# Batch 0 of a fused attention and FP4 feed-forward kernel: where the weight splits, the scales, the quantising of tiles and GpSimd's rounding stand among the steps

## The reference, cut to what matters

```python
xn = _layernorm(x)                                   # x: (8, 512, 512)
qkv = xn @ Wqkv_w.T + Wqkv_b                         # 16 q heads, 8 k heads, 4 v heads of 256
p = softmax(q1 @ k1.T) - lam * softmax(q2 @ k2.T)    # causal, differential attention
o = einsum('bhqk,bkhe->bqhe', p, v)
s = (o * rsqrt(mean(o*o) + EPS) * subln_w * (1 - LAMBDA_INIT)) @ out_w.T + out_b
a, w = quant_dequant_mxfp4(xn), quant_dequant_mxfp4(weight)   # blocks of 32, shared power of two
g = silu(a @ w.T + bias)
out = x + s * g
```

## Time and profile before

| | |
|---|---|
| median of 3 runs | 1618.49 us (1616.91 to 1618.52) |
| the profiled execution's own time | 1619.56 us |
| its span, first to last instruction | 1617.8 us |
| busy share of PE, DVE, ACT, POOL | 92%, 70%, 54%, 53% |

### The profile page before, as it was taken

The page is one execution under the profiler, slowest core; times in us unless marked ns, Lnnn a source line. Parts: engine busy times, 40 slices in busy tenths (PEclk is TensorE's granted clock), DMA queues, the critical chain, the costliest instruction groups (busy, mean ns, idle before and its releaser), DMA issues.

```text
span 1617.8 us, 27497 instructions
## 1 busy us (share of the span) xinstructions
PE 1485.5 (92%) x8956; PEld 866.4 (54%) x8972; DVE 1134.8 (70%) x2657; ACT 877.0 (54%) x2474; POOL 852.6 (53%) x1587
## 2 busy tenths in 40 slices
PE   4676878999899998999999998999999998999978
PEld 2343445456565565556564555555654555655644
DVE  6778677757777677757777578767777577775661
ACT  5456766346653566346663476436663466534651
POOL 2455445655455554655556555655546554554443
PEclk9888989999999999999999999999999999999999
DMA  8144543234433334234532344334442344323332
GB/s 260 38 102 92 114 84 68 47 98 81 84 63 95 79 61 94 64 85 86 97 73 47 96 82 88 65 98 73 79 88 54 93 85 89 69 59 77 67 72 72
DMA packets 382352, 134.23 MB, mean 83 GB/s; under 512 B 361856, under 2 KB 365952, under 8 KB 382208
## 3 DMA queue, kind: packets, MB, share of 16 engines
q1 hardware_dynamic: 382208, 132.46, 38.8%
HBM read 35.41 MB, written 8.39 MB: 27 GB/s over the span
## 4 chain that ended last, share of the span: by engine, by line
PE 51%; DVE 15%; ACT 12%; POOL 9%; issue 7%; DMA 4%; SPq 1%; ACTq 0%; POOLq 0%; DVEq 0%
PE ps L527 14%; PE ps L529 14%; PE ps L528 14%; ACT pp L694 4%; DVE ps L1004 3%; DVE qkv L962 3%; PE ps L598 2%; PE ps L596 2%; PE ps L597 2%; ACT qkv L671 2%; ACT ph L703 2%; DMA pT<-ph 2%; ACT on L716 1%; DMA out_x<-res 1%; DVE ph L1016 1%
## 5 line engine op out<-in xcount | busy, mean ns | idle before, releaser
L694 ACT ACTIVATE pp<-ps,row 128x384 f32<-128x384 f32 (+3 forms) x512 | 268.0, 524 | 294.4 <-DVE row L1004 293.1
L1208 POOL TENSOR_TENSOR row<-row,small 128x1 f32<-128x1 f32 x256 | 141.0, 551 | 422.7 <-ACT pp L694 422.7
L527 PE MATMUL ps<-xT,wqkv 128*128 128x512 f16 x768 | 294.7, 384 | 14.3 <-DVE wqkv L902 7.4
L1004 DVE CUSTOM_DVE_ANT_0 ps<-ps,mask,ssc 128x384 f32<-128x384 f32 (+3 forms) x512 | 280.3, 552 | 31.4 <-PE ps L598 29.7
L529 PE MATMUL ps<-xT,wqkv 128*128 128x512 f16 x768 | 294.3, 383 | 0.0
L528 PE MATMUL ps<-xT,wqkv 128*128 128x512 f16 x768 | 294.2, 383 | 0.0
L1016 DVE SCALAR_TENSOR_TENSOR ph<-pp,small,ph 128x128 f16<-128x128 f32 (+3 forms) x256 | 152.0, 594 | 121.6 <-ACT ph L703 119.4
L527 PE MATMUL ps<-qkv,pT 128*128 128x256 f16 x640 | 177.7, 278 | 54.1 <-DMA pT<-ph 52.4
L962 DVE SCALAR_TENSOR_TENSOR qkv<-ps,bsc,qkv 128x512 f16<-128x512 f32 x192 | 143.3, 749 | 101.8 <-ACT qkv L671 100.9
L703 ACT ACTIVATE ph<-pp,small 128x128 f16<-128x128 f32 (+3 forms) x256 | 141.4, 552 | 128.5 <-DVE pp L1010 126.7
L527 PE MATMUL ps<-wout,heads 128*128 128x512 f16 x512 | 194.3, 380 | 2.5 <-DVE qkv L962 1.7
(11 more groups left out here) (133 smaller groups left out, 2979.0 us busy)
## 6 DMA issues: line engine op xcount, KB each, us to landing
xres<-in_x SPq DMA_DIRECT2D x32, 256.0 KB, 3.5
out_x<-res SPq DMA_DIRECT2D x32, 256.0 KB, 2.3
wqkv<-in_wqkv SPq DMA_DIRECT2D x15, 512.0 KB, 6.6
xin<-in_x SPq DMA_DIRECT2D x7, 1024.0 KB, 5.9
vbias<-in_bv SPq DMA_DIRECT2D x32, 128.0 KB, 3.2
pT<-ph SPq DMA_TRANSPOSE x256, 2.7
wout<-in_ow SPq DMA_DIRECT2D x7, 512.0 KB, 4.5
heads<-on SPq DMA_TRANSPOSE x128, 3.2
```

Source lines behind the costliest of these rows:

```text
L527: mm(out, ah, bh, start=start and j == 0, stop=False)
L694: run(out, sc_ps[u][:, m, 0:w], ACT.Exp, bias=ebias[:, u, m:m + 1], scale=-1.0, accum_out=psum_l[:, n % 6, m:m + 1]).then_inc(exp_done, 1)
L1004: nc.vector.tensor_tensor_reduce(sc, sc, mask[:, S - w:S], ssc[:, c:c + 1], BIG, ALU.add, ALU.min, ebias[:, u, m:m + 1]).then_inc(max_done, 1)
```

## The change

It touches only the setup and batch 0, apart from two waits.

- Each weight's low part (`w_low`, `o_low`) is done by DVE one step after ACT's high part, ahead of `normalised_lo`, where before both stood at the end of one step. The high parts move too: those of Wqkv by up to two steps in either direction, and those of out_w up to two steps earlier.
- The four parts of a tile are no longer done two per step in ten steps: ops 0 to 3 stand in one step and ops 4 and 5 two steps later (`TILE_AT`). Tiles 1 (its second half) to 7 are in steps 1 to 15; the setup does 6 parts in place of 12.
- POOL rounds a tile one step after DVE's ops 0 to 3, behind its small operations for the softmax.
- `norms` is no fill any more: it stands in `attend`, writes the unused half of an output bank, and comes at steps 4, 8 and 20 in place of 5, 11 and 23. The squares it sums are asked for at steps 3, 7 and 20. DVE copies its result in the step after.
- The layer norm of batch 1 moves from steps 9 to 12 to steps 15 to 18 on DVE; POOL's root is one step behind DVE's statistics, in the same step as ACT's use of it. The high parts of x move to steps 17 to 20.
- In the setup ACT does all four layer norms first, DVE all four low parts of x, and PE runs ten extra matmuls ("warm") ahead of fill 0; `norm 1` stands behind fill 0.
- The feed-forward weight is loaded into `heads`, not `gate`. The last out_w tile is loaded twice, once for its square and once for its split.

```diff
-X_STEP = 5
+X_STEP = (6, 5)
...
-SQ_STEP = {8: 0, 9: 1, 10: 2, 11: 3, 12: 6, 13: 7, 14: 8, 15: 9, **{WT + p: 13 + p for p in range(OP - 1)}, WT + OP - 1: 21}
-LOAD_O = {**{p: 10 + p for p in range(OP - 1)}, OP - 1: 19}
-NORM_STEP = {2: 5, 3: 11, 4: 23}
-W_SPLIT = {5: 0, 6: 1, 7: 3, 8: 6, 9: 7, 10: 9, 11: 11, 12: 13, 13: 14, 14: 15, 15: 17}
+SQ_STEP = {8: 0, 9: 0, 10: 1, 11: 2, 12: 4, 13: 5, 14: 5, 15: 6, **{WT + p: 12 + p for p in range(OP)}}
+LOAD_O = {p: 9 + p for p in range(OP)}
+SUM_STEP = {3: 3, 7: 4, 20: 5}
+NORM_STEP = {4: 3, 8: 4, 20: 5}
+W_SPLIT = {5: -1, 6: 1, 7: 3, 8: 5, 9: 7, 10: 9, 11: 10, 12: 12, 13: 13, 14: 15, 15: 17}
+OUT_SPLIT = {0: 22, 1: 23, 2: 24, **{p: 23 + p for p in range(3, OP)}}
...
+TILE_AT = {1: (None, 1), 2: (1, 3), 3: (3, 5), 4: (7, 9), 5: (9, 11), 6: (11, 13), 7: (13, 15)}
...
-AQ_STEP = WQ_STEP[NT - 1] + 2
-OUT_SPLIT = {p: 24 + p for p in range(OP)}
+AQ_STEP = WQ_STEP[NT - 1] + 1
...
-SETUP = [("norm", 0), ("norm", 1), ("fill", 0), ("fill", 1), ("fill", 2), ("fill", 3), ("fill", 4),
+SETUP = [("norm", 0), ("warm", 10), ("fill", 0), ("norm", 1), ("fill", 1), ("fill", 2), ("fill", 3), ("fill", 4),
...
                 wait(pe, on_lo, n - 1)
+                if n in NORM_STEP:
+                    norms(junk[u], NORM_STEP[n])
...
+                for t in range(5, WT):
+                    if W_SPLIT[t] == n - 1:
+                        w_low(t)
+                for p in range(OP):
+                    if OUT_SPLIT[p] == n - 1:
+                        o_low(p)
+                if n - 1 in NORM_STEP:
+                    dve.wait_ge(on_hi, n)
+                    take(junk[(n - 1) % 2], 4)
                 if n:
                     normalised_lo(n - 1)
...
-                if b == 0:
-                    for t in range(5, WT):
-                        if W_SPLIT[t] == s:
-                            w_low(t)
...
                 for c in range(SETUP_PARTS, 32) if b == 0 else ():
-                    if c % 4 == 1 and part_at(c)[0] == s:
+                    if c % 4 == 1 and part_at(c)[0] == s - 1:
...
-                for k in norm_at(b, s) if b + 1 < B else ():
+                for k in norm_at(b, s if b else s - 1) if b + 1 < B else ():
```

More of the change, by code:

```diff
@@ L390, in load_w, with load_o @@
                 sp.dma_start(w_src(t), wqkv_d[t].rearrange("p a n -> p (a n)")).then_inc(ld_w[t], 16)
[L392 to L396, removed]
+            def load_o(p, src):
+                sp.dma_start(src, ow_d[p].rearrange("p m n -> p (m n)")).then_inc(ld_ow[p], 16)
             sp.dma_start(bcol, bcol_d).then_inc(ld_small, 16)
@@ L429, in _ @@
                 load_w(t)
[L430 to L432 removed]
+            sp.dma_start(wq, fw_d.rearrange("(k p) h -> p k h", p=P)).then_inc(ld_fw, 16)
             for t in range(8, 12):
@@ L477, in _ @@
                     if LOAD_O[p] == s:
-                        load_o(p)
-                if s == X_STEP and b + 1 < B:
+                        load_o(p, o_sum(p))
+                if n == AQ_STEP + 3:
+                    for j in range(2):
+                        sp.wait_ge(aT_done[j], 16)
+                    load_o(OP - 1, o_src(OP - 1))
+                if s == X_STEP[b > 0] and b + 1 < B:
                     sp.wait_ge(q_done, (b + 2) * NT if b else NT)
@@ L730, in layer_norm @@
                     .then_inc(xn_done, 1)
[L732 to L735, removed]
+            for k in range(NT):
+                layer_norm(k, k)
+                x_hi(k)
             square(0)
+            square(1)
             act.wait_ge(su_lam, 1)
             run(lamv[:, 2:4], lamv[:, 0:2], ACT.Exp).then_inc(su_exp, 1)
-            for k in (2, 3):
-                layer_norm(k, k)
-                x_hi(k)
             w_high(0)
-            for t in range(1, 4):
-                square(t)
+            square(2)
+            square(3)
             w_high(1)
@@ L766, in _ @@
             fill(FIRST[7])
+            w_high(5)
             for n in range(NSTEPS):
@@ L875, in o_squares, with take, scales @@
                 nc.vector.tensor_copy(wnorm[:, 17:18], bsum[:, 16:17]).then_inc(su_in, 1)
-            def scales(i, sums, free=None):
+            def take(sums, count):
+                link(nc.vector.tensor_copy(bound[:, 0:count], sums[:, 0:count]))
+            def scales(i):
                 lo, hi = ((0, 1), (1, 4), (4, 8), (8, 12), (12, 16))[i]
-                link(nc.vector.tensor_copy(bound[:, 0:hi - lo], sums))
-                if free is not None:
-                    nc.vector.memset(apart, 0.0).then_inc(free, 1)
                 power_scale(scl[:, lo:hi], bound[:, 0:hi - lo], 10, half=4)
@@ L973, in fill @@
                     tt(bank, bank, fbias[:], ALU.add).then_inc(biased, 1)
[L974 to L979, removed]
-                        o_scales(bank[:, 0:2])
                 elif kind == "last" and LAST_PIECES[j][g][1] < OC:
@@ L1050, in _ @@
                 layer_norm(k, k, 0)
+            for k in range(NT):
+                x_lo(k)
+            squares(0)
             dve.wait_ge(ld_lam, 16)
@@ L1077, in _ @@
             fill(FIRST[1])
+            w_low(3)
+            fill(FIRST[2])
             quantise_early(1)
-            w_low(3)
-            for m in range(2, 5):
-                fill(FIRST[m])
-                quantise_early(2)
+            fill(FIRST[3])
+            quantise_early(1)
+            fill(FIRST[4])
             maxima(0, 1)
@@ L1094, in _ @@
             dve.wait_ge(su_norm, 3)
-            scales(2, ps[:, 6, 0:4])
+            take(junk[0], 4)
+            scales(2)
             score_scales(1)
@@ L1128, in _ @@
                         gating(f)
+                if SUM_STEP.get(n) == 5:
+                    o_squares()
+                elif n in SUM_STEP:
+                    squares(SUM_STEP[n])
                 prepare(b, s, "maxima")
+                for t in range(5, WT):
[7 more added lines that the diff above has]
+                    take(junk[(n - 1) % 2], 4)
                 if n:
                     normalised_lo(n - 1)
+                if n - 1 in NORM_STEP:
+                    if n < 16:
+                        scales(NORM_STEP[n - 1])
+                        score_scales(NORM_STEP[n - 1] - 1)
+                    else:
+                        o_scales()
                 for f in PLAN[n]:
```

80 lines of the change are left out of this document (39 added, 41 removed).

## The result

The changed kernel takes 1607.26 us (median of 5 runs, 1603.83 to 1612.23) against 1618.49 (5 runs, 1615.47 to 1620.75) before: a ratio of 0.9937, 95% interval 0.9913 to 0.996. It is faster by 11.2 us, where 22 were forecast. The profiled execution took 1606.69 us, with a span of 1604.9.

What follows compares the result with a forecast made beforehand. PE bounds the kernel overall, but hand-overs between DVE, ACT and POOL bound batch 0. Setup -11, steps 0 to 15 -12, steps 16 to 21 +8, steps 22 to 31 -7: -22 us, median about 1596, own range 1586 to 1603, whole 1584 to 1609.

Steps and rivals of the forecast that it cites:

- steps 16 to 21: Batch 0, where DVE and ACT work arrives and ACT waits for POOL's root: +8 us, from +4 to +12.
- the setup: Everything until step 0: earlier fill 0, less tile work, a shorter scale chain; -11 us, from -7 to -14.
- steps 22 to 31: Batch 0's end: `o_scales` leaves and 5 of 8.0 us of waits for `o_high` go; -7 us, from -2 to -10.
- steps 0 to 15: Batch 0's first steps: mainly less DVE idle time; -12 us, from -4 to -18.
- the +2: Steps 0 to 15: two more POOL rounds in the loop stretch DVE operations beside them, +2 us.
- +3.3 and -1.1: Steps 16 to 21, ACT's work: four layer norms and a high part of x arrive (+3.3 us), a square leaves (-1.1).
- I expect only 2.5 us of this: Setup: fourth low part of x comes about 4.9 us earlier, of which 2.5 us is gained; bounds 0 and 4.9.
- I take +1.5: Setup: `norm 1` behind fill 0 on PE, with `w_low(1)` and fill 2 behind it, costs 1.5 us; bounds 0 and 5.
- -5.5 + 1.5: Setup: tile 1's quantising leaves its place ahead of the first scores (-5.5 us); `norm 1` behind fill 0 costs +1.5.
- -4.5: Setup, 44.57 us to step 0: ops 0 to 3 replace a whole tile (-1.5), round after the scale chain (-3).
- Rival 3: Loop: a round and a `w_low` lock each other in seven steps, 1.3 us each; +9, 1605 us; chance 0.08.
- Rival 1: Loop: waits only change place, only the setup's -11 remains; 1607 us, from 1603 to 1611; chance 0.17.

Runs made afterwards that it cites:

- the second run with later bias loads: Changed kernel with layer norm a step later, norm 1 first, two more warm matmuls, bias loads behind x's transposes, bias wait at fill 6: 1596.36 us (0.9854).
- the first run with later bias loads: Changed kernel with layer norm a step later, norm 1 first, eight more warm matmuls, bias loads behind x's transposes: 1598.96 us (0.9888).

## Why the prediction was off, step by step

The mechanisms of the sum were mostly right, and sizes failed: steps 16 to 21 cost 15.8 us, not 8, the setup gave 6.4 us, not 11, and steps 22 to 31 gave 10.6, not 7.

**Right.** That the page's 92% hides a batch 0 whose bound is the hand-overs between DVE, ACT and POOL, and that time saved there is not given back later: the part behind batch 1 changed by 0.9 us. That steps 0 to 15 lose 12 us: they lost 12.5. DVE was idle 13.3 us in them (106.54 - 93.20), against 13.4 forecast from the 0.84 us a step of steps 16 to 21. DVE operations beside a round were stretched by 6.3 us in all in these steps, and by 4.2 before (what each takes beyond the same operation away from a round, summed), as the +2 had it. The two mechanisms behind the gain were shown one at a time: the low parts' hand-over (8.6 us of the stretch when undone) and the rounds (7.9). Together this is more than the 12.5, so they overlap. Of the sum's four terms, only this one ended within its bounds; the setup (-6.4) and steps 22 to 31 (-10.6) missed theirs by 0.6 us each, steps 16 to 21 by 3.8. A setup of the same code varied by 1.4 to 1.6 us, so its 0.6 means little.

**"Steps 16 to 21 ... it will also wait in four steps for POOL's root ... some 1 us each, half of it hidden. I take +6.5 + 1.5 = +8."** This term failed by its size: +15.8, outside its bound of +12. The wait was 2.0 us each (7.9 in four), and taking the hand-over apart gave back 5.4 us of the stretch, where the sum had 1.5 for it. I had counted it on ACT alone; but the high part of x stands behind the layer norm, and DVE's low part of x in the same step behind that, so DVE stood still too (6.3 us) and began the next step late. With the hand-over a step later, the stretch took 40.5 us, near the 38.2 that the sum gives. This is 5.4 of the 7.8 us that the term was off. For the rest there is ACT's work: it rose by 5.9 us in the stretch (25.28 to 31.20), where I had +3.3 and -1.1. Four squares of weight tiles stand in it before and after, so that none was lost, and the high part of one more Wqkv tile now falls inside its bounds. That this is what the last 2.4 us are is how I read it, and no run tells it apart.

**"I expect only 2.5 us of this (bounds 0 and 4.9)."** Fill 0 came 0.35 us earlier. DVE's fourth low part did come 4.8 us earlier, at 11.87, but what counts is the transpose behind it. SP in the changed kernel:

```profile
9.86 9.23 SPq L434 DMA_TRANSPOSE xT<-gate  x2
```

The first was issued at 9.86 and landed 9.4 us later, behind the loads in the queues. Its issue alone kept SP for 7.3 us (4.3 with the bias loads behind it), and the second was issued at 17.2 only, nearly as late as before (17.4), to land 4.4 us later. I had moved the transpose on the engine that asks for it and not on the queue that carries it. Moving the bias loads behind it brought the landing to 18.5 us, though step 0 gained only 0.5 of this.

**"`norm 1` now stands behind fill 0 ... I take +1.5, with bounds 0 and 5."** It cost 2.5 us, and fill 0 at the lower clock another 1.7, as the two runs on it showed. The warm matmuls, which I gave nothing in the sum, gave nothing that shows; with PE idle for 4.1 us behind them, fill 0 was slow all the same.

In these executions the 4.6 us missing from the setup lie in three places: 2.2 at the start of fill 0; 1.4 between it and the first scores (-2.6 in place of -5.5 + 1.5); and 1.0 from there to step 0 (-3.5 in place of -4.5), where a 4-column operation of the scale chain still takes 1.00 us (L839 at 49.68), now beside POOL's low part of v.

**"A round stretches what DVE does beside it ... +2."** This was about right (4.2 us before, 6.3 after). Rival 3, full blocking at every `w_low`, did not come about, but its mechanism was hardly put to the test: of eleven in the loop, one took 2.35 us, beside the round of step 0, 1.07 more than the other ten with 1.28, which is near the 1.3 of the rival. Those in a step with a round came some 2.4 us before it (69.13 and 71.54, 83.06 and 85.46) and did not meet it.

**"Steps 22 to 31: -7."** It was -10.6, just outside the bound of -10. The step that failed is "so I count 5 of them": I had set 5 of 8 us for the eight waits for `o_high`. Undoing the hand-over costs 6.4 us there, and the kernel before with it alone gains 8.9.

**Rival 1** (the waits only change place) comes nearest in time, 1607, but by the wrong sum: the loop did gain, 7.3 us, and the setup gave 6.4, not 11. Its mechanism was in part there: against the 20.1 us of waits that went, the one in `p_lo` grew by 13.1 (9.7 to 22.8 us), and DVE's idle time fell by 12.6 us in all. The measured 1607.26 lies outside the forecast's own range (to 1603) and inside the whole one (to 1609). The forecast erred in that two errors of one sign, 4.6 and 7.8 us, met one of 3.6 us the other way. Of the 13.8 us at the start of batch 1 the medians show 11.2; the rest lies in the part behind, whose length varies by more.

The account of the change is then: the weights' hand-over about -14 in the loop (14.1 when undone), the rounds -8, the layer norm's hand-over +7, some 5 us of DVE work moved in from the setup, and a setup of -6.4. They sum to some -16, against -13.8 measured; they are not quite independent. The first alone, on the old order, gave 16.1 in the loop. The 5 us are DVE's busy time in the loop, 162.7 us before and 167.9 after. What the new place of the `norms` matmuls is worth was tried in no run.

## What to carry to other kernels

When two in-order engines finish a step by handing a result from one to the other, move the receiver's half a step later and ahead of what it must wait for anyway: on the kernel before, this alone was worth 16.1 us of the loop's 213.6, of 20.1 us of waits that it removed. Expect some of the waiting to turn up at the next hand-over, as it did in `p_lo`. For each chain of hand-overs that a change creates within one step, follow it to its last receiver, since every engine on it pays; here POOL's root, placed one step later to spare POOL, held ACT and DVE both. A transfer that is asked for earlier is only as early as the queue ahead of it.

## What the runs showed of the hardware

The steps of batch 0 repeat almost to the hundredth: with edits elsewhere, step 4 took 5.02 or 5.03 us in eight of these executions. The setup doesn't, as said above, and neither does the part behind. From the start of batch 1 to the end, with the same work, the profiled executions took from 1342.89 us (before) and 1343.78 (after) to 1350.45 (low parts in the same step) and 1354.81 (the second run with later bias loads). PE's granted clock was 1.00 before and 0.99 in the other three. This is why a gain of 2 us ahead of batch 1 is seen in a trace and not in the median. Over whole executions of one kernel, a lower mean granted clock mostly goes with a longer time: of the six of that last kernel, the three at 0.989 and 0.990 took 1593.2 to 1593.7 us, and the three at 0.983 to 0.986 took 1599.0 to 1605.3. What sets the clock in the later part, and whether it is all of the difference, was not tried and stays open.

In the setup PE's clock was high at fill 0 only where matmuls led up to it. In the changed kernel the ten warm matmuls begin at 13.63 us with 0.59 to 0.63 us each, and the last begins at 17.21 and takes 0.38. Then PE is idle for 4.08 us, and the clock falls:

```profile
20.50:27.20 6.70, 5.54 (x15) 2.38 (x16) 0.00 (x1) 0.00 (x0) 1.90 (x2) 0.50 0.96 340
```

Fill 0, from 21.66, ran at 0.63 us a matmul until about 27 us. These are the two levels of the clock, 1.2 and 2.4 GHz: the matmuls follow each other at 0.43 us in the one case (22.04 and 22.47) and 0.21 to 0.22 in the other. Of the five executions with the ten alone, all began fill 0 with a matmul of 0.58 or 0.59 us. In three the clock had risen within the ten and fell in the 3.8 to 4.1 us of idle PE; in two (rounds in the same step, `norm 1` first) it had not risen before fill 0 at all. In the four with two or eight more behind `norm 1` it was up at `norm 1`, before the added ones, and fill 0 began at 0.38 us. Why the same ten raise it in some executions and not in others, no run tells.

The clock also fell while fill 2 ran, in four executions, with PE idle for 2.4 to 2.7 us before it (without warm matmuls, low parts in the same step, rounds in the same step, and the first run with later bias loads). It didn't in the changed kernel, after 2.37 us. Fill 2 took 4.1 to 4.5 us in the four, and 2.8 there.

The Trainium skill (TensorE: Matmul & The Clock Gate, "HAM oscillation — how this bites in real kernels") tells of a kernel that falls back to the lower clock in its waits for DMA; the trace of the changed kernel agrees, with the 4.08 us wait for the transpose, the granted clock of 0.50 and the 0.63 us matmuls behind it.
